# An attention iteration with some steps of TensorE, ScalarE and VectorE in another order, and one load issued earlier

## What is computed

```
x = x + tanh(g_xattn[0]) * cross_attention(layernorm(x), ctx, ctx)      # 16 heads of 16, softmax
x = x + tanh(g_ffn[0])   * ffn0(layernorm(x))                           # relu(h)^2, ternary weights, low-rank term
x = x + tanh(g_xattn[1]) * align(ctx, layernorm(x))                     # distances, DTW, backtracking, scatter
x = x + tanh(g_ffn[1])   * ffn1(layernorm(x))                           # quantised activations, gelu
```

## Time and profile before

| what | value |
|---|---|
| runs | 1814.77, 1813.73, 1809.11 us; median 1813.73 |
| span of the profiled execution | 1810.7 us |
| TensorE busy | 1379.4 us (76%) |
| VectorE busy | 1489.1 us (82%) |
| ScalarE busy | 1135.9 us (63%) |
| GpSimd busy | 644.9 us (36%) |

### The profile page before, as it was taken

How to read it: one execution, slowest core, us unless ns; L and a number is a source line. 1 busy time by engine, 2 the same in 40 slices (tenths; PEclk the granted TensorE clock), 3 DMA queues, 4 the chain that set the end, 5 groups by cost and what they waited for, 6 DMA issues and landing times. The chain is left out here.

```text
span 1810.7 us, 37501 instructions
## 1 busy us (share of the span) xinstructions
PE 1379.4 (76%) x11461; PEld 1067.0 (59%) x11461; DVE 1489.1 (82%) x4194; ACT 1135.9 (63%) x2463; POOL 644.9 (36%) x1094
## 2 busy tenths in 40 slices
PE   4899999999999999999999984233332004899996
PEld 4577878888888888888888764000001003666664
DVE  7777877878878787788877753999998998999995
ACT  4567677776777767777677662243334002999997
POOL 3333343433434334343343322200000003787785
PEclk7999999999999999999999996555555556999999
DMA  6444544445444454444544311322220002223321
GB/s 173 137 128 115 149 123 118 137 122 154 123 117 139 120 154 123 118 141 122 152 125 120 99 36 28 96 60 61 60 42 8 0 0 84 74 89 98 96 77 48
DMA packets 322942, 179.56 MB, mean 99 GB/s; under 512 B 93793, under 2 KB 318193, under 8 KB 322802
## 3 DMA queue, kind: packets, MB, share of 16 engines
q1 hardware_dynamic: 322802, 178.07, 35.2%
HBM read 122.91 MB, written 50.33 MB: 96 GB/s over the span
## 5 line engine op out<-in xcount | busy, mean ns | idle before, releaser
L1031 DVE TENSOR_REDUCE nmax<-s 128x2 f32<-128x512 f32 x512 | 327.5, 681 | 7.6 <-PE s L465 6.6
L737 ACT ACTIVATE pts<-s 128x512 f32<-128x512 f32 x512 | 282.3, 617 | 75.0 <-PE s L482 74.8
L1143 POOL TENSOR_TENSOR r<-rl 128x512 f32<-128x512 f32 x128 | 133.4, 1042 | 260.8 <-ACT rl L767 217.9
L465 PE MATMUL s<-kst,qst 96*128 96x256 bf16 x1024 | 158.7, 276 | 10.9 <-DVE nmax L1031 6.9
L482 PE MATMUL s<-qst,kst 128*128 128x256 bf16 x1024 | 160.3, 276 | 8.7 <-ACT pts L737 7.2
L1421 PE MATMUL gate<-diag,one 128*128 128x512 f16 x35 | 21.2, 607 | 171.9 <-DVE left L1512 171.9
L767 ACT ACTIVATE rl<-wb,fscl 128x256 f32<-128x256 f32 x256 | 108.0, 477 | 64.8 <-PE wb L568 64.8
L564 PE MATMUL wb<-x2l,wfcT 128*128 128x256 f32 x512 | 143.3, 302 | 0.7 <-ACT dd L789 0.7
L1000 DVE TENSOR_TENSOR r2l<-r,r2h 128x512 fp32r<-128x512 f32 x128 | 88.6, 692 | 66.0 <-POOL r L1143 40.3
L496 PE MATMUL oacc<-pts,vw 128*32 128x256 f32 x2048 | 137.9, 387 | 5.3 <-ACT pts L737 5.2
L431 PE MATMUL wb<-wprT,r2l 128*128 128x256 f32 x512 | 130.5, 293 | 6.9 <-DVE r2l L1000 6.9
(11 more groups left out here) (304 smaller groups left out, 4630.9 us busy)
## 6 DMA issues: line engine op xcount, KB each, us to landing
kst<-k_parts_dram SPq DMA_DIRECT2D x384, 64.0 KB, 2.6
qst<-q_parts_dram SPq DMA_DIRECT2D x384, 64.0 KB, 2.4
k_parts_dram<-kp SPq DMA_DIRECT2D x32, 384.0 KB, 5.4
q_parts_dram<-qp SPq DMA_DIRECT2D x32, 384.0 KB, 3.1
xin<-in_x_dram SPq DMA_DIRECT2D x32, 256.0 KB, 2.8
cT_raw<-in_ctx_T_dram SPq DMA_DIRECT2D x32, 256.0 KB, 5.4
xres<-in_x_dram SPq DMA_DIRECT2D x32, 256.0 KB, 3.1
cin<-in_ctx_dram SPq DMA_DIRECT2D x32, 256.0 KB, 4.7
```

Source lines behind the costliest of these rows:

```text
L465: last = pe.matmul(s1[h % 2][:, t, :], qst[b.p][0:MAXROW, h, t * P:t * P + P], kst[b.p][0:MAXROW, h, :], start=True, stop=True)
L737: act.activation(pt[h % (2 * HPG)], s2[h % 2][:], ACT.Exp).then_inc(e["expd"], 1)
L1031: v.tensor_reduce(nmax[:, T * h:T * h + T], s1[h % 2][:], AX.X, ALU.max, negate=True)\
L1143: pool.tensor_tensor(r2[:], rl[:, k % 2], rl[:, k % 2], ALU.mult)\
```

## The change

Nothing is added or removed in what is computed; the same instructions are issued, some in another order, and one wait is split.

- SP: `load_ctx_products(z)` is issued ahead of `load_x`, `load_res` and `load_ctx` and no longer behind them.
- TensorE: `scores1(s, 0, 2)` goes between `turn_x` and `keys`, and no longer behind `turn_on`. `proj(y, 0)` starts when three of the four square steps are done and waits for the fourth ahead of slice f = 6. `scores2(i, 6, 8)` goes ahead of `scores1(s, 6, 8)`.
- ScalarE: the fourth `square` moves from the end of an iteration to behind `xT_copy` in the next one (there the batch is called y). `exps(i, 4, 8)` run in one series; `yT_copy` and then `values_copy` come behind it. `half_copy` goes ahead of `middle_part` of the queries.
- VectorE: the fourth `low_squares` moves from the end of an iteration to behind `x_low` in the next one.

```diff
@@ SP iteration @@
+                if there(z):
+                    load_ctx_products(z)
                 if there(x):
                     load_x(x)
                 if there(i):
                     load_res(i)
                     load_ctx(i)
-                if there(z):
-                    load_ctx_products(z)
@@ TensorE proj @@
                 if t == 0:
-                    w("sq_low", 4 * (b.n + 1), 4 * NB)
+                    w("sq_low", 4 * b.n + 3, 4 * NB)
                     w("x_low", b.n + 5), w("max_split", b.n + 3)
                 for f in range(FT):
+                    if t == 0 and f == FT - 2:
+                        w("sq_low", 4 * (b.n + 1), 4 * NB)
@@ TensorE iteration @@
                 if there(a):
                     turn_x(a)
+                if there(s):
+                    scores1(s, 0, 2)
+                if there(a):
                     keys(a)
                 if there(z):
                     turn_on(z)
                 first = at(i, -1)
-                if there(s):
-                    scores1(s, 0, 2)
...
                     values_proj(s)
+                if there(i):
+                    scores2(i, 6, 8)
+                if there(s):
                     scores1(s, 6, 8)
...
-                if there(i):
-                    scores2(i, 6, 8)
@@ ScalarE iteration @@
                 if there(a):
                     xT_copy(a)
+                if there(y):
+                    square(y, 3)
+                if there(a):
                     kh_copy(a)
...
-                    exps(i, 4, 6)
-                if there(s):
-                    values_copy(s)
-                if there(i):
-                    exps(i, 6, 8)
+                    exps(i, 4, 8)
                 if there(y):
                     yT_copy(y)
+                if there(s):
+                    values_copy(s)
                 if there(z):
                     xh2_copy(z)
+                if there(y):
+                    half_copy(y)
                 if there(a):
                     middle_part(a, "q_rem", qr, qp, "q_parts_mid")
-                if there(y):
-                    half_copy(y)
...
                     relu(z, 3)
-                    square(z, 3)
@@ VectorE iteration @@
                 if there(a):
                     x_low(a)
+                if there(y):
+                    low_squares(y, 3)
+                if there(a):
                     k_remainder(a)
...
-                if there(z):
-                    low_squares(z, 3)
```

More of the change, by code:

```diff
@@ L813, in iteration @@
                     copy_group(i, 0)
-                    exps(i, 4, 6)
+                    exps(i, 4, 8)
+                if there(y):
+                    yT_copy(y)
                 if there(s):
                     values_copy(s)
-                if there(i):
-                    exps(i, 6, 8)
-                if there(y):
-                    yT_copy(y)
                 if there(z):
                     xh2_copy(z)
+                if there(y):
+                    half_copy(y)
                 if there(a):
                     middle_part(a, "q_rem", qr, qp, "q_parts_mid")
-                if there(y):
-                    half_copy(y)
                 if there(i):
```

## The result

The changed kernel takes 1792.46 us (median of four runs, 1790.66 to 1793.27) beside 1812.99 us for the kernel before (four runs, 1809.11 to 1814.77): a ratio of 0.9882, 95% interval 0.9864 to 0.9901. The profiled execution has a span of 1791.5 us where before had 1810.7. All 19.2 us lie in the attention phase: the first load of the alignment phase is issued at 1110.2 instead of 1129.4, and the rest takes as long as before.

What follows compares the result with a forecast made beforehand. TensorE was taken to bound the attention phase, with only its small waits to remove. Gains of 16.6 (steady), 7.3 (four early iterations) and 1.5 (ends) make 25.4: 1810.7 - 25.4 + 3.0 = 1788.3 us, range 1779 to 1802.

Steps and rivals of the forecast that it cites:

- The bound: TensorE bounds the attention phase at clock 1.00; gains come only from its small waits, 31 us over 28 iterations at most.
- (1) cD_raw: On ScalarE: fetched first, cD_raw lands in 2.8 us and leaves no wait; at 6.8 it costs 1.3 in such an iteration.
- (2) and (3), the start: Start of a TensorE iteration: proj at +2.67 instead of +3.18; of the 0.51, 0.28 is lost at scores1(2,4), 0.23 stays.
- Rival A: The start of an iteration gives nothing: later maxima take back proj's head start; 1794.7 us, chance 0.17.
- B: More goes: the maximum does not hold scores1, 0.28 more per iteration, or the ramp gives its 3; 1779 us, chance 0.14.
- (4), the middle: ScalarE and TensorE mid-iteration: xh waits for VectorE until +15.99; hpart at +17.52 instead of +18.04, 0.62 earlier in all.
- Rival D: cD_raw still lands late or the middle stays tied to VectorE's chain; only the start's 0.23 stays: 1807 us, chance 0.11.
- (5), half_copy ahead of middle_part: ScalarE late in an iteration: low_copy about 0.06 later, minus 0.06; later q stacks cost 0, covered by 1.7 us of slack.
- rival C: Slower, the stacks become late: scores1(0,2) waits for the last qst load; 1859 us, chance 0.06.
- The end of the phase: The two or three iterations behind 1018 us gain between nothing and about 1 us each.
- The start of the phase: The iteration before 111.1 us gains between nothing and about 1 us; 1.5 was taken together with the last iterations.
- the 3.0 us that I added: Distance of the profiled span, 1810.7, below the median, 1813.7, kept and added to the forecast time.

Runs made afterwards that it cites:

- e2: The changed kernel with the maxima of heads 0 and 1 ahead of k_remainder on VectorE: 1782.82 us, ratio 0.9824 to the kernel before.
- e6: The kernel before with only the middle's new order on ScalarE and TensorE, half_copy ahead of middle_part included: 1816.70 us, ratio 1.0019.
- e4: The changed kernel with the load of cD_raw back behind the other three: 1814.16 us, ratio 0.9998 to the kernel before.
- e5: The kernel before with only the start changed: scores1(0,2) ahead of keys, proj's wait split, fourth square and its low part moved: 1809.86 us, ratio 0.9976.
- e1: The changed kernel with middle_part of the queries back ahead of half_copy: 1784.91 us, ratio 0.9840 to the kernel before.
- e7: The kernel before with only the wait of proj split, the fourth square awaited ahead of slice 6: 1809.34 us, ratio 0.9981.
- b2: b1 with scores1(s, 0, 2) of the first three batches back behind keys on TensorE: 1774.79 us, ratio 0.9787 to the kernel before.
- b1: The changed kernel with the edits of both e1 and e2: 1775.75 us, ratio 0.9794 to the kernel before.
- e3: The kernel before with only the load of cD_raw moved ahead of the other three: 1801.44 us, ratio 0.9931.
- b3: b2 with maxima(4,6) behind ln2 on VectorE and scores1(6,8) behind turn_xh2 on TensorE: 1775.30 us, ratio 0.9791 to the kernel before.

## Why the prediction was right, and where it wasn't

*The bound.* Right. TensorE has work in 98% or more of both stretches at granted clock 1.00, and every gain in the period was a small wait that went. (The 1.2 us of waits in 28 iterations are 34 us, not the 31 of the text; nothing hangs on it.) Right too was to take one length for all iterations, since what the edits remove is what varies: 21 of the 23 steady iterations of after last 31.79 to 31.93, those of before 31.95 to 32.49.

*(1) cD_raw.* Right, and it was the part that carried the rest. Landing is 2.9 in the median where 2.8 was taken from xin's place, against 4.8 in its own. The landing goes by the place in the series: xin, now second, takes 3.1 (2.8 as the first), xres, third, 4.6 (3.1 as the second), and cin, the fourth in after and the third in before, 4.7 in both. The Trainium skill (DMA: Bandwidth & Descriptors, Queues, rings and completion order) has each DMA engine consume descriptors in ring order; the landings agree with that. My text gave this part no price of its own in the sum, and took the early iterations to differ from the steady ones by this wait: they did, 31.87 and 31.88 now.

*(2) and (3), the start.* Right to 0.05 us: proj 0.54 earlier where 0.51 was forecast, 0.30 lost at scores1(2,4) where 0.28 was, and out_proj 0.28 earlier where 0.23 was. The split wait inside proj costs nothing there, as taken: the products on both sides of it start at 753.82 and 753.93, at the usual pitch. Rival A, in which nothing of it stays, is out. So is B for this kernel, since the maximum does hold scores1; e2 shows that its 0.3 can be had by one exchange on VectorE.

*(4), the middle.* Right: xh still waits for VectorE (+15.95 against +15.99), values and hpart start 0.02 from their forecast. Rival D, the middle tied to VectorE's chain, is out: hpart came 0.5 earlier. The sum gives no price of its own to the order. The runs give this: without the load it brings hpart 0.11 forward (e6 against before) or sets it 0.05 back (e4 against e5), and the load is worth 0.48 at hpart with the new order of start and middle and 0.17 with the old.

*(5), half_copy ahead of middle_part.* The wrong term, "minus 0.06". It measured 0.30 (e1). The rows of before from which it could have been worked out are these of ScalarE and TensorE, in the iteration of the earlier trace rows:

```profile
779.81 0.55 ACT L760 ACTIVATE hrows<-wb 32x128 bf16<-32x128 f32 x2 [0.31 <-PE wb L526]
...
781.64 0.84 ACT L789 ACTIVATE dd<-wb,aa 128x256 f32<-128x256 f32 x2 [0.35 <-PE wb L540]
782.37 0.38 ACT L754 ACTIVATE lowt<-wb 128x256 fp32r<-128x256 f32 x1
```

```profile
783.77 0.39 PE L568 MATMUL wb<-lowt,low 128*128 128x256 f32 x1
```

The q step, 0.64 long, had run before the wait of hrows, which hid part of it. The change puts it behind that wait, where only the 0.35 idle ahead of dd can hide it. So lowt comes 0.64 - 0.35 = 0.29 later against the matmuls. There was no slack for that: VectorE's lowt and the product follow lowt at once, and even in before the product stood 0.17 behind its neighbour (783.60 to 783.77) instead of 0.12. I followed the slack of the q parts on SP's queue at length (it held: from T4 to T31 scores1(0,2) nowhere waits for a stack, so rival C is out) and not the chain of the same engine two steps on. The period came out at 31.88 against 31.55, and most of this is the term: it measured 0.30 where 0.06 was in the sum, and 27 iterations by 0.24 are 6.5 of the 9.0 us that the early and steady stretches fell short together. Without the term the forecast was 31.49, and e1 has 31.58.

*The end of the phase.* Also wrong, the other way: 6.0 us gained where the sum has 0.7 for the first of these iterations and at most 2 for the rest. The last proj of the phase, in before and in after (start us, us, then the wait), and the stretch of both its halves:

```profile
1108.55 0.58 PE L431 MATMUL wb<-wprT,r2l 128*128 128x256 f32 x1 [4.74 <-DVE r2l L1000]
```

```profile
1108.50:1114.80 6.30, 6.25 (x32) 6.07 (x32) 0.00 (x0) 0.00 (x0) 0.00 (x0) 0.60 0.00 0
```

```profile
1090.50 0.38 PE L433 MATMUL wb<-wprT,r2l 128*128 128x256 f32 x1 [2.83 <-DVE r2l L1004]
```

```profile
1090.50:1096.10 5.60, 5.55 (x32) 5.35 (x32) 0.70 (x2) 0.00 (x0) 1.04 (x1) 0.70 0.00 0
```

```profile
1105.71 0.38 PE L433 MATMUL wb<-wprT,r2l 128*128 128x256 f32 x1 [2.84 <-DVE r2l L1002]
```

The last line is e7's, which has the split and nothing else. In after the wait is 1.91 shorter, since proj no longer needs the fourth square to begin, and the 32 products take 0.70 less, at granted clock 0.70 instead of 0.60. The split acts earlier on, where three waits of 0.43 to 0.87 for r2l are gone. e7 shows it alone: 4.2 us with an unchanged period, and 5.7 of the 6.0 us of this stretch. I had costed the split at 0 to -0.1 inside the steady loop and never asked where the wait for r2l is really met, which is where the pipeline empties.

*The start of the phase.* Forecast as 0 to 1 gained, measured 1.0 lost. TensorE in the iteration that begins at T1 (20.4 in before, 20.2 in after), the first with scores1, before and after:

```profile
24.11 0.58 PE L361 MATMUL wb<-cTl,wkTh 128*128 128x256 f32 x1 [3.05 <-POOL cTl L1132]
...
30.84 1.03 PE L465 MATMUL s<-kst,qst 96*128 96x256 bf16 x4 [3.81 <-DMA qst<-q_parts_dram]
```

```profile
30.58 1.03 PE L467 MATMUL s<-kst,qst 96*128 96x256 bf16 x4 [9.24 <-DMA qst<-q_parts_dram]
```

scores1(0,2) now stands ahead of keys and waits for a stack that is still being written; keys, ready since 24, waits behind it. But b2, which takes that away, gains no more than 1 us over b1. The start's new order and the load can be told apart in the traces by where they first act. At T3 nothing of the load or of proj has acted yet: T3 is 78.5 to 80.2 in five kernels with scores1(0,2) behind keys there (before, e3, e6, e7, b2), but 83.8 in b3, and 82.2 to 82.8 in five with it ahead (after, e1, e2, e4, e5), but 80.5 in b1. From T3 to T4, where the first cD_raw is needed, the seven kernels with its load issued first take 28.3 to 30.5 us and the five others 32.0 to 33.7; ScalarE waits for it 5.8 us there in before, 1.2 in after. So in after the start is likely to have lost some 3 us and the load to have given back about 3. The 1.0 left over is less than the spread of single executions: before and e7 are the same up to T4 and differ by 2.4 there, and from 54 to 111 us the granted clock was 0.94 in before and after, 0.88 in e7, 0.85 in e1 (T4 113.3) and 0.97 in b2 (108.1). What the start costs here stays open to that extent.

*The total.* The forecast of 1788.3 is 4.2 us from the median. That is partly luck: the sum was 25.4 and the spans differ by 19.2, since the gain was put 6.5 us too high on term (5), 2.5 too high in the rest of the same iterations and 1.5 at the start of the phase, and 4.3 too low at its end; and of the 3.0 us that I added for the distance between span and median, 1.0 was there. The direction and the range rested on the steps that held.

## What to carry to other kernels

When a step is moved past a wait on its own engine, the wait no longer hides it: take the idle times that the engine has behind the new place off its length, one by one, and what remains arrives at whoever waits for the last step. Where a chain meets the bounding engine at two places, an edit inside the chain that advances only the first meeting gains almost nothing (b3); follow it to the last meeting. And parts of one change are not to be costed singly: the load was worth 12.5 us on the old order and 21 on the new, so test the undoing of each part beside the part alone. Where a part by itself loses, look for the exchange in it that does it, by a start that moved, before the whole part is blamed: in e6 it was, by the traces, half_copy's place.

## What the runs showed of the hardware

I had not expected TensorE's clock to matter in this phase. It is 1.00 from T4 to T31, but the 32 products of the last proj, behind a wait of 4.74 us, took 6.30 us at granted clock 0.60, and 5.60 at 0.70 behind 2.83; the same products stand 0.12 apart in the steady loop, or 3.8 us for 32. At the start of the phase, behind a wait of 9.24, products stood 0.21 apart (31.84 to 32.05) at granted clock 0.50 (30.6 to 35.0), which is the 1.2 GHz of the two levels, and four small matmuls took 0.85 to the next group (48.82 to 49.67) where 0.44 is usual. The kernel before has the same 0.21 there (24.49 to 24.70), behind a wait of 3.05. So a wait of TensorE at the end of the phase can cost more than its own length: between before and after, 1.9 us less of waiting came with 0.7 us less of work. All twelve kernels can be compared at this place. Behind 4.73 to 4.75 us (before, e3, e6) the 32 products took 6.24 to 6.27; behind 2.82 to 2.84 they took 5.54 to 5.58 in eight kernels, but 6.67 in e2, at granted clock 0.56. The length of the wait is thus not all that counts, and what else does is not shown.
